# Cross attention and feed-forward of a decoder layer merged into one stage, with the gate and up products taken batch by batch

## The reference

```python
x = x + xattn(layernorm(x), ctx)      # q = (clip(round(v / s + z), 0, 255) - z) * s on both, then matmul
x = x + ffn(layernorm(x), w_gate, w_up, w_down)

def fake_quant(t, axis):
    s = max(max(abs(t), axis) / 127, 1e-8)
    return clip(round(t / s), -128, 127) * s

def qlinear(x, w):                    # tokens by rows of x, weights by rows of w
    return einsum('bsh,oh->bso', fake_quant(x, -1), fake_quant(w, 1))

gate, up = qlinear(x, w_gate), qlinear(x, w_up)      # 1024 -> 2752
return qlinear(silu(gate) * up, w_down)              # 2752 -> 1024
```

## Time and profile before

| | us |
|---|---|
| median of 3 runs (1672.59 to 1675.81) | 1673.52 |
| the profiled execution | 1680.11 |
| its span | 1678.3 |
| TensorE, matmuls busy | 1408.4 (84%) |
| VectorE busy | 1320.8 (79%) |
| ScalarE busy | 932.4 (56%) |
| GpSimd busy | 931.9 (56%) |

### The profile page before, as it was taken

The page is one execution under the profiler, slowest core; times in us unless marked ns, Lnnn a source line. Parts: engine busy times, 40 slices in busy tenths (PEclk is TensorE's granted clock), DMA queues, the critical chain, the costliest instruction groups (busy, mean ns, idle before and its releaser), DMA issues. The chain is left out here.

```text
span 1678.3 us, 17914 instructions
## 1 busy us (share of the span) xinstructions
PE 1408.4 (84%) x5550; PEld 728.3 (43%) x5576; DVE 1320.8 (79%) x1641; ACT 932.4 (56%) x1375; POOL 931.9 (56%) x767
## 2 busy tenths in 40 slices
PE   6999577788888987768798788888999994999798
PEld 3443233444444444344454454444434442444443
DVE  6585898898898889989998898889147655777684
ACT  1211568767767755877766766765223223556670
POOL 0000678798797877889998898898200000333300
PEclk9999798999998998987999999999999996999899
DMA  7596332443442532333673682674373203588504
GB/s 273 201 352 255 93 126 97 161 151 106 153 160 101 168 107 95 112 127 103 229 253 98 221 272 87 229 244 157 133 290 142 75 26 72 151 187 193 125 0 175
DMA packets 155468, 264.38 MB, mean 158 GB/s; under 512 B 76560, under 2 KB 94096, under 8 KB 149552
## 3 DMA queue, kind: packets, MB, share of 16 engines
q1 hardware_dynamic: 151056, 236.27, 43.3%
q10 hardware_dynamic: 4320, 27.00, 4.4%
HBM read 207.60 MB, written 38.60 MB: 147 GB/s over the span
## 5 line engine op out<-in xcount | busy, mean ns | idle before, releaser
L1073 DVE TENSOR_TENSOR_SCAN hbuf<-decay,hbuf 128x512 f32<-128x512 f32 x512 | 613.2, 1214 | 51.3 <-ACT decay L773 51.0
L773 ACT ACTIVATE decay<-delta,chan_sb 128x512 f32<-128x512 f32 x512 | 348.8, 687 | 293.5 <-DVE hbuf L1073 292.1
L586 PE MATMUL turn<-ident,hbuf 128*128 128x128 f32 x2048 | 338.1, 294 | 183.3 <-DVE hbuf L1073 141.0
L586 PEld LDWEIGHTS turn<-ident,hbuf 128*128 128x128 f32 x2048 | 256.2, 150 | 455.6 <-DVE hbuf L1073 215.4
L1087 DVE SCALAR_TENSOR_TENSOR acc<-turn,pn,acc 128x512 f32<-128x512 f32 x360 | 263.9, 733 | 44.7 <-PE turn L586 43.6
L907 POOL TENSOR_TENSOR hbuf<-wout,sx 128x512 f32<-128x512 f32 x172 | 213.5, 1276 | 15.0 <-DVE wout L1060 15.0
L907 POOL TENSOR_TENSOR hbuf<-du,sx 128x512 f32<-128x512 f32 x172 | 213.1, 1273 | 1.7 <-DMA sx<-bt_scratch 1.7
L928 POOL TENSOR_TENSOR acc<-acc,part 128x512 f32<-128x512 f32 x120 | 153.3, 1277 | 56.5 <-ACT part L783 56.4
L1776 PE MATMUL bank<-codes,wout 128*128 128x512 bf16 (+1 forms) x690 | 153.2, 382 | 1.7 <-PEq L1190 1.0
L568 PE MATMUL bank_g<-wout,codes 128*128 128x512 f32 x256 | 138.0, 626 | 0.0
L498 PE MATMUL bank_u<-wout 128*128 128x512 f32 x224 | 110.9, 614 | 2.7 <-DMA wout<-in_wu 1.8
(11 more groups left out here) (215 smaller groups left out, 2119.8 us busy)
## 6 DMA issues: line engine op xcount, KB each, us to landing
wout<-in_woutT SPq DMA_DIRECT2D x48, 512.0 KB, 4.6
sx<-bt_scratch SPq DMA_DIRECT2D x86, 256.0 KB, 3.7
codes<-in_wg SPq DMA_DIRECT2D x8, 2048.0 KB, 8.9
ubuf<-u_scratch SPq DMA_DIRECT2D x16, 1024.0 KB, 6.7
wout<-in_w_gate SPq DMA_DIRECT2D x26, 512.0 KB, 4.8
wout<-in_w_up SPq DMA_DIRECT2D x26, 512.0 KB, 4.3
raw_d<-in_w_down ACTq DMA_DIRECT2D x8, 1376.0 KB, 6.7
b_more<-bt_scratch SPq DMA_DIRECT2D x42, 256.0 KB, 3.5
```

The source lines that it names most:

```text
L586: last = pe.transpose(turn[t % 2][:, j * P:j * P + P], hbuf[:, s % 4, j, t * P:t * P + P], ident[:, :])
L773: act.activation(decay_bank[q % 2][:, :], delta[:, G % 2, j, :], ACT.Exp, scale=a_col(GD * (G % GROUPS) + j, n)).then_inc(dA_done, 1)
L1073: dve.tensor_tensor_scan(h, decay_bank[q % 2][:, :], h, 0.0, ALU.mult, ALU.add).then_inc(scan_done, 1)
```

## The change

One function `tail` with one block takes the place of `attend` and `feed_forward`.

1. Stages: `STAGES` keeps the first 8. What is left of tiles 5, 6 and 7 stands at fixed units inside the loop of products, on each engine.
2. The loop runs over 44 units (chunk, batch), first all chunks of batch 0, then all of batch 1. Each unit loads its pair of weights anew: 88 transposes in place of 44, still in a ring of three. The first three pairs are issued before `store_x2(0)`.
3. Products use four banks, two units deep, in place of eight and four slots. The other four serve attention, the peaks and the spreads.
4. w_down's tiles have fixed units (`WD_UNITS`); its raw rows have two slots used as `RAW_SLOT` says, its turned codes lie by output tile in two halves, and the down product walks them as four runs of 128 columns.
5. Batch 0's peak is turned after unit 24 and its scales spread after unit 26; its codes are made from unit 28 on. Batch 1's peak is turned inside the down product, and its codes are made beside it.
6. The down product takes token tiles in pairs, (0,1), (2,3), (4,5), then 6 and 7, in banks that alternate.
7. All buffers lie by hand in one allocation `space` and in `wout`, which brings waits of their own (on `out_mm`, `cross_mm`, `x2_stored`).

The core of the diff (the functions not shown are as before, or with other names of buffers):

```diff
-    starts = list(range(NT - 1)) + [None, NT - 1] + [None] * 3
-    STAGES = [tuple(starts[i - lag] if i >= lag else None for lag in range(4)) for i in range(len(starts))]
+    STAGES = [(i if i < NT - 1 else None,) + tuple(i - lag if i >= lag else None for lag in (1, 2, 3)) for i in range(NT)]
+    UNITS = BATCH * OC
+    UR = 4
+    WD_UNITS = [(3, 9), (12, 17)] + [(17 + 4 * i, 21 + 4 * i) for i in range(6)]
+    RAW_SLOT = (0, 0, 1, 0, 1, 0, 1, 0)
+    HID_AT = 28
+    def at(u):
+        return u % OC, u // OC, rows(u % OC)
+    def bank_gate(u):
+        return bank[2 * (u % 2)]
+    def bank_up(u):
+        return bank[2 * (u % 2) + 1]
@@ on SP @@
+            load_attn(3)
+            for u in range(WT):
+                load_wT(u)
+            store_x2(0)
...
+            for u in range(UNITS):
+                if u + WT < UNITS:
+                    load_wT(u + WT)
+                if u == 3:
+                    store_x2(6)
+                if u == 10:
+                    store_x2(7)
+                for t in wd_last(u - 1):
+                    turn_wd(t)
@@ on TensorE @@
+            def products(u):
+                c, b, r = at(u)
+                pe.wait_ge(wT_load[u % WT], 32 * (u // WT + 1))
+                if u % OC == 0:
+                    pe.wait_ge(codes_kept, TT * (b + 1))
+                if u < 2:
+                    pe.wait_ge(x1_done, 7 + u)
+                for m, (to, free, done) in enumerate(((bank_gate(u), gate_scaled, gate_mm), (bank_up(u), up_scaled, up_mm))):
+                    if u >= 2:
+                        pe.wait_ge(free, u - 1)
...
+            for u in range(UNITS):
+                products(u)
+                if u == 5:
+                    turn_code3(5)
+                if u == 6:
+                    turn_code(7)
+                if u == 7:
+                    row_sums(7)
+                    cross(7)
+                if u == 9:
+                    turn_code3(6)
+                if u == 14:
+                    turn_code3(7)
+                if u == 24:
+                    turn_peak(0, bank_p[0])
+                if u == 26:
+                    spread_ih(0, bank_p[1])
+                if u == 40:
+                    spread_sd()
+            down((0, 1), 0, 11)
+            turn_peak(1, bank[0])
+            down((0, 1), 11, 16)
+            spread_ih(1, bank[1])
+            down((0, 1), 16, OC)
+            down((2, 3), 0, OC)
...
@@ on ScalarE @@
+            for u in range(UNITS + 1):
+                if u == 8:
+                    row_fix(7)
+                if u < UNITS:
+                    silu(u)
+                for t, q in wd_pieces(u):
+                    round_d(t, q)
+                if u >= 1:
+                    size(u - 1)
+                if u == 2:
+                    affine3_of(5)
+                if u == 3:
+                    affine(7)
+                if u == 6:
+                    keep_codes(5)
+                    affine3_of(6)
+                if u == 7:
+                    copy_codeT(7)
...
@@ on VectorE @@
+            for u in range(UNITS + 2):
+                if u < UNITS:
+                    scale_products(u)
+                if u >= 2:
+                    raise_peak(u - 2)
+                if u == 1:
+                    stage_d(5)
+                if u == 2:
+                    stage_b_first(7)
+                    stage_c(6)
+                if u == 3:
+                    stage_d_last(5)
+                if u == 4:
+                    stage_b(7)
+                if u == 5:
+                    stage_d(6)
+                if u == 7:
+                    stage_d_last(6)
+                if u == 8:
+                    stage_c(7)
+                if u == 10:
+                    stage_d(7)
+                if u == 12:
+                    stage_d_last(7)
...
+                if u == 25:
+                    hid_scales(0, bank_p[0])
+                if HID_AT <= u < UNITS:
+                    scale_hid(u - HID_AT, 0)
+                    hid_codes(u - HID_AT)
+                for t in wd_first(u + 2):
+                    scales_d(t)
```

More of the change, by code:

```diff
@@ new lines, in tail @@
+        x2t = [part(3072 + 1024 * i, 1024) for i in range(2)]
+        yT = part(6144, 4096).rearrange("p (w c t) -> p w c t", w=2, t=P)
+        gs = [part(6144 + 512 * i, 512) for i in range(2)]
+        us = [part(7168 + 512 * i, 512) for i in range(UR)]
+        ctx_q = part(10240, 8192).bitcast(BF16).rearrange("p (b k h) -> p b k h", b=BATCH, k=KC)
+        code = part(18432, 1024).bitcast(BF16).rearrange("p (i h) -> p i h", i=2)
+        code3 = part(19456, 1024).bitcast(BF16).rearrange("p (i h) -> p i h", i=2)
@@ new lines, in tail @@
+        hid1 = part(20480, L * HID_OWN).rearrange("p (c t) -> p c t", t=L)
+        ih_row = [part(28160, 512), gs[0]]
+        q0 = [part(28672 + 256 * b, 256).bitcast(BF16) for b in range(BATCH)]
+        late = wout[:, OC // 2:DC, :].rearrange("p r j -> p (r j)")
+        raw_d = [late[:, 0:INTER], part(3072, INTER)]
+        code_d = late[:, 3072:3072 + OC * P // 2].bitcast(BF16)
+        peak = [late[:, 4480:4992], part(29184, 512)]
+        res = [late[:, i * H:i * H + H] for i in range(2)]
@@ L1326, in _ @@
                 store_x2(i)
[L1327 to L1332, removed]
+            for u in range(UNITS):
[7 more added lines that the diff above has]
+                    turn_wd(t)
             for i in range(XR):
                 sp.wait_ge(x2_stored[i], 16 * ((NT - 1 - i) // XR + 1))
+            sp.wait_ge(wd_plain, NP * JT)
+            for i in range(2):
+                load_x2(i)
+            for i in range(NT):
+                store(i)
+                if i + 2 < NT:
+                    load_x2(i + 2)
+            for i in range(2):
+                sp.wait_ge(out_stored[i], 16 * (NT // 2))
         @block.tensor
@@ L1402, in turn_code3 @@
                           start=True, stop=True).then_inc(s3_spread, 1)
+            def products(u):
[8 more added lines that the diff above has]
+                        pe.wait_ge(free, u - 1)
+                    for k in range(KC):
+                        last = pe.matmul(to[0:r, :], wT[:, u % WT, m, k, 0:r], keep.codes[:, k, b * L:b * L + L],
+                                         start=(k == 0), stop=(k == KC - 1))
+                    last.then_inc(done, 1)
@@ new lines, in turn_peak, with spread_ih @@
+            def turn_peak(b, to):
+                pe.wait_ge(peak_done, OC * (b + 1))
+                if b == 0:
+                    pe.wait_ge(x2_done, 2 * NT)
+                else:
+                    pe.wait_ge(gate_scaled, UNITS)
+                for i in range(TT):
+                    last = pe.transpose(to[:, i * P:i * P + P], peak[b][:, i * P:i * P + P], keep.ident[:, :])
+                last.then_inc(peak_turned, 1)
+            def spread_ih(b, to):
+                pe.wait_ge(sh_step, 3 * (b + 1))
+                if b == 1:
+                    pe.wait_ge(up_scaled, UNITS)
+                for i in range(TT):
+                    last = pe.matmul(to[:, i * P:i * P + P], ih[:, TT * b + i:TT * b + i + 1].to_broadcast([P, P]),
+                                     keep.ident[:, :], start=True, stop=True)
+                last.then_inc(ih_spread, 1)
@@ L1992 @@
+                result(i)
 class Keep:
@@ L2023, in program @@
               attn_dram)
[L2024 to L2025 removed]
+        tail(nc, keep, x, yT_dram, attn_dram, context, scales, wq_dram, w_down, x2_dram, out)
 def laid_out(inputs):
```

681 lines of the change are left out of this document (325 added, 356 removed).

## The result

The changed kernel takes 1696.52 us in the median of 4 runs (1685.82 to 1703.89), the kernel before 1674.66 (1672.59 to 1681.56). The ratio is 1.011 with a 95% interval from 1.0079 to 1.014: about 1% slower, clear of the noise, where 1662 us and faster had been forecast. The profiled execution took 1703.81 us, its span is 1702.0. Ratios in this document leave out executions more than 1.5% above the fastest of their kernel: three of ten in e12 (1705.00, 1706.41 and one of 2861.53 us), two of ten in e13, and none elsewhere.

The account below looks back on a forecast made before the run. TensorE was taken to set the pace except in two holes. 204.2 - (162.2 + 12 + 13.6 + 6) gave 10.4 us earlier; with -2.3 for the down product and +1.4 at the end, net -11.3 us: 1662, range 1651 to 1671.

Parts of the forecast that it names:

- The weights are loaded twice: Units 17 to 32: SP needs 17.2 us per four units, TensorE 13.8; 13.6 us lost, between 0 and 17.6.
- the clock rival: TensorE's granted clock falls in every stall, 2.2 us a fall; ten falls cost 22 us, time 1684; chance 0.08.
- The start: Products begin at 1389.65 in place of 1424.11, 34.5 us earlier; six transposes ahead of store_x2(0) cost nothing.
- Early VectorE stalls: Units 0 to 16: TensorE waits on VectorE and ScalarE with two-unit banks; 12 us, between 6 and 18.
- Late units: Units 28 to 43: batch 0's codes on VectorE and ScalarE's waits for code_d turns cost 6 us, between 0 and 14.
- DMA keeps up: Transposes overlap loads in the products, no group above TensorE's 13.8 us; gain 28 to 31 us, time 1644; chance 0.23.
- Down product: Straight behind the last unit, 77.5 us in place of 79.8; the new walk over w_down's codes costs nothing.
- The end: After the down product, both halves of tile 7 finish together, two more VectorE operations before the last store: +1.4 us.
- the tiles' own pieces: TensorE's remaining turns, spreads, row sums and cross(7) among the products, 7.1 us at full clock.
- the bounds: Ends of the early, DMA and late terms taken together, 1638 us at the best for the whole kernel.
- SP's transposes stretch: slower: SP's queue, units 17 to 40: a pair takes 4.6 us, a group 25; time 1706; chance 0.12.

Follow-up runs that it names:

- e12: Changed kernel with units reordered so chunks 15 to 21 share one weight pair for both batches, 37 pairs for 44; 1683.39 us, ratio 1.0043 to the kernel before.
- e13: e12 with batch 0's rounding also written as scalar_tensor_tensor; 1688.47 us, ratio 1.0084 to the kernel before.
- e2: Changed kernel with only the first load of w_down into each of its two slots, six of eight dropped (values wrong); 1671.92 us, ratio 0.9993.
- e3: Changed kernel with one weight transpose per unit, gate's used for up too, 44 for 88 (values wrong); 1669.82 us, ratio 0.9969.
- e4: Changed kernel with the 88 weight transposes replaced by plain loads of the same bytes (values wrong); 1668.53 us, ratio 0.9957.
- e1: Changed kernel with w_down's loads issued from SP's queue, ahead of the turn of code_d, instead of ScalarE's queue; 1701.76 us, ratio 1.0144.
- e5: Kernel before with each chunk's weight pair loaded once per batch, 88 transposes for 44, in the same ring of three; 1707.03 us against 1679.28, ratio 1.0156.
- e11: Changed kernel with only batch 0's rounding rewritten as scalar_tensor_tensor with a broadcast column; 1700.2 us, ratio 1.0118 to the kernel before.
- e9: e4 with batch 0's rounding rewritten as scalar_tensor_tensor with a broadcast column; 1671.28 us, ratio 0.9962 to the kernel before.

## Why the prediction was wrong

The step that failed is the one headed "The weights are loaded twice": four groups at 3.4 us, 13.6 in all, the excess of SP's 17.2 us over TensorE's 13.8. In its place stand 49.0 us of waits for weights and half-clock time behind them. TensorE is busy for 178.8 us after, and for 168.4 to 174.5 in e2, e3 and e4, where weights wait 7 to 9 us, so the clock's part is 4 to 10 us. Two errors made up the size.

*A sum in place of an order.* The step compared what SP and DMA have to do in four units with what TensorE has to do. It left out that the ring now reaches three units ahead, 10.4 us, while a turn of code_d stands in SP's queue in front of the next pair. e1 shows this bare: its transposes issue in 1.31 us in the median, SP issues for 19 us a group and not 17.2, and each group waits 4.5 to 6.2 us, with periods of 21 to 23 us. e5 shows the doubled pairs in the old order: 22.3 us of waits. The prices were too low besides: 2.55 us a pair was read from one stretch with nothing else in flight, where whole stages show 3.05 (e2, e3) and 3.5 beside loads from the other queue (after), and a load of w_down 5.6 for 4.07. By the prediction's prices the products after hold 41 x 2.55 + 8 x 3.9 + 8 x 4.07 = 168 us of DMA; 215 were measured. But e1 has 188 and loses nearly as much (products 3.4 us shorter), so the DMA sum alone isn't what TensorE waited for. How the kernel after would run with a deeper ring stays open.

*Where it counts.* Only the groups of units 17 to 32 were taken as over-full. The periods of four units, by VectorE's scaling of gate, are after 22.3, 29.3, 14.1, 22.9, 16.6, 36.6, 19.6, 30.0, 19.0 and 15.7 us from unit 1 on, and in e4 22.3, 30.5, 14.1, 16.5, 16.1, 16.1, 17.5, 19.0, 19.0 and 15.7. So the transposes' loss is in units 13 to 16 (6.4 us) and 21 to 32 (20.5, 2.1 and 11.0). From unit 33 on the periods are the same, though one wait for weights of 5.4 us still stands there. The loss comes in blocks, five of them with a granted clock of 0.50, not as about 1 us a unit as the forecast said when it gave the clock rival 0.08.

The other terms:

- *The start.* Products 35.4 us earlier against the first projection (forecast 34.5). The six transposes ahead of `store_x2(0)` cost nothing that shows. Right.
- *Early VectorE stalls*, 12 us: 0.36 + 3.92 + 3.83 + 1.51 = 9.6 of idle time and about 4 of half clock, 14 in all. Right in place and nearly in size; the one behind `turn_code(7)` came 0.7 us shorter than drawn.
- *Late units*, 6 us. Mis-sized, but it did not decide: rounding was priced at 0.34 us from rows where GpSimd was idle (0.42 each, with overlapping ends) and takes 1.38 beside it. That is 1 us a unit for 16 units. After, it is mostly hidden behind the weights (e11), and e2 to e4 show it bare: in units 25 to 40 their groups are 16 us over 4 x 13.8. This is why even with weights in time the gain was 5 to 11 us and not the 28 to 31 of the rival in which DMA keeps up.
- *Down product*: 77.5 forecast, 78.4 measured, straight behind the last unit; the walk over four runs of 128 columns costs nothing that can be seen. *The end*: 1.4 longer forecast, 5.8 us for 4.6 measured. Right.
- Two slips of the working change nothing: the tiles' own pieces add up to 7.0 us and not 7.1, and the bounds give 1637 at the best and not 1638.

Of the rivals, "SP's transposes stretch: slower" (1706, chance 0.12) came nearest, in time and in place. It was to decide from a pair of 3.1 us in the mean, and over units 17 to 40 a pair took SP 3.5 us, waits for a place left out. But the median issue stayed at 1.31 us: the stretch is in a few issues of up to 11.9 us, in the blocks in which the transfers took long. And it isn't needed for the loss: in e1 a pair takes 2.5 us and TensorE waits in every group all the same. "DMA keeps up" did not come about in the kernel after. The clock rival holds in part: seven falls, of which two stand in the early stalls and five at waits for weights, for the ten that it wanted.

The Trainium skill's sentence in Advanced Engine Details and Errata, section X-Bar Transpose (TRN2), quoted in the prediction, doesn't hold in these runs: exchanging transposes for plain loads of the same bytes cut a pair from about 3.05 us to 1.8 and the waits from 49.0 us to 8.0.

The Trainium skill's page SBUF — State Buffer, section SBUF: two separate sides, says that VectorE, in a fast mode that uses both ports or with two operands in SBUF, and GpSimd take a shared pair of ports as an exclusive lock, for the whole instruction. The trace agrees for the rounding (1.38 us ending 0.3 us behind GpSimd's multiply, 0.42 or 0.43 without it), and for its other form with a second operand in SBUF (1.64 and 0.75 us, e9). It was a reason to doubt a price read beside an idle GpSimd.

What stays open: why single transposes needed 16 and 23 us in the kernel after while the DMA engines moved 50 to 60 GB/s at a share above 1 (1494 to 1506 us). With the loads in the same queue it didn't come back (e1), but the products were hardly shorter, so it isn't shown whether it cost anything by itself. Nor do the runs separate SP's issues, the DMA engines and the reach of the ring: every run that relieved one relieved another. Why the mixer's length differs by 12 us between profiles of the same instructions is open too.

## What to carry to other kernels

A restructuring that closes idle time on the busiest engine by moving data a second time has to be weighed on the queue that issues it, and as a sequence and not only as a sum: here 50 us of TensorE's holes were bought with 22 more pairs of transposes, and DMA's share went from 72% to 90%. Write down how long the buffers in hand last, and what the queue must issue before the next one is filled; here that was 10.4 us against up to 16. Loading the data twice into the same ring also halves its reach. Price a transfer from a stage in which everything that will fly beside it is in flight, not from a clean stretch. Price an elementwise operation with its neighbour running; an operation moved beside GpSimd's work can cost three times its row.

## What the runs showed of the hardware

- The same transfers (82 transposes of 256 KB, eight of code_d, eight loads of 1.41 MB) hold the DMA engines for 215 us from two queues and for 188 from one (e1). By estimate a pair goes from 3.05 to 3.5 us of all 16 engines and a load from 4.1 to 5.6 when the loads come from the other queue.
- A DMA share above 1 can go with 50 to 60 GB/s for 12 us; here the share says that packets are in flight and not that bytes move. The stretch, kernel after:

```profile
1494.00:1500.00 6.00, 0.91 (x5) 0.20 (x2) 1.35 (x2) 3.15 (x4) 1.43 (x2) 0.85 1.14 50
1500.00:1506.00 6.00, 0.00 (x0) 0.00 (x0) 0.00 (x0) 0.00 (x0) 0.00 (x0) 0.50 1.22 60
```

- SP spends 1.31 us (median) on issuing a transpose of 128 x 1024 bf16 and 0.43 us on a plain load of the same bytes.
- VectorE's rounding of 128 x 512 (f32 in, bf16 out) takes 0.42 us alone and 1.38 beside GpSimd's multiply, and GpSimd's multiply 1.27 alone and 1.56 in that unit; a scalar_tensor_tensor with a broadcast operand is held too (0.75 alone, 1.64 beside it).
